# Trainium2 case: five late stages of a transformer kernel turned from waited-for passes into streams, with a new threshold search and one-hot tables

## The reference, cut to what matters

```python
x = x + ffn2(_layernorm(x))     # h = gelu(x @ tern(W_fc).T), exact gelu; LN(h)*w+b; @ tern(W_proj).T
                                # 128 -> 512 -> 128; tern(W) = sign(W)*min(round(|W|/mean|W|), 1)
x = x + xattn3(_layernorm(x))   # softmax((x @ W + b) @ y^T) @ y, y = 64 context rows per batch
x = x + ffn3(_layernorm(x))     # below; 8 experts, 128 -> 512 -> 128

route_prob = jax.nn.softmax(xf @ Ws + bs, axis=-1).T      # [8, 4096]
route_vals, routes = jax.lax.top_k(route_prob, 512)       # each expert takes 512 tokens
h = jax.nn.gelu(jnp.einsum('ekd,edf->ekf', xf[routes], W1) + b1[:, None, :])
out = (jnp.einsum('ekf,efd->ekd', h, W2) + b2[:, None, :]) * route_vals[..., None]
final = zeros.at[routes.reshape(-1)].add(out.reshape(-1, D))
```

## Time and profile before

| what | value |
|---|---|
| median of 3 runs (lowest to highest) | 5028.88 us (5028.64 to 5030.45) |
| profiled execution, its own time | 5030.85 us |
| its span, first to last instruction | 5029.1 us |
| granted TensorE clock, mean | 0.918 |
| busy: PE, DVE, ACT, POOL | 84%, 73%, 56%, 44% |

### The profile page before, as it was taken

One profiled execution on the slowest core, in us unless ns is written; L12 is line 12 of the kernel. 1 busy time (PEld: TensorE's weight loads), 2 busy tenths in 40 slices (PEclk: granted clock), 3 DMA queues, 4 the chain that ended last, 5 costly groups with the idle time before them and its releaser, 6 DMA issues. The chain is left out here.

```text
span 5029.1 us, 113839 instructions
## 1 busy us (share of the span) xinstructions
PE 4220.7 (84%) x40234; PEld 2422.8 (48%) x40619; DVE 3670.4 (73%) x8812; ACT 2816.3 (56%) x5023; POOL 2236.8 (44%) x1403
## 2 busy tenths in 40 slices
PE   8969999999999999999999999999999546456426
PEld 5635555545555555555554555555555325244314
DVE  7878878878888888888887887888887453554440
ACT  3436666666666666666666666666666455342001
POOL 0026555555555555555555555555555001300025
PEclk9989999999999999999999999999999668685558
DMA  1023222322232222322223222232222000000202
GB/s 38 1 67 68 53 59 56 75 60 58 54 77 58 60 56 57 77 56 58 59 54 76 62 55 58 55 76 59 58 54 54 16 11 1 5 0 9 68 6 29
DMA packets 186665, 245.77 MB, mean 49 GB/s; under 512 B 88549, under 2 KB 129255, under 8 KB 186088
## 3 DMA queue, kind: packets, MB, share of 16 engines
q1 hardware_dynamic: 180904, 239.95, 20.5%
q0 software_dynamic: 5632, 4.33, 0.7%
HBM read 41.13 MB, written 14.30 MB: 11 GB/s over the span
## 5 line engine op out<-in xcount | busy, mean ns | idle before, releaser
L1229 POOL TENSOR_TENSOR f_rot_a<-f_rot_a,f_norm 128x1024 f32<-128x1024 f32 x384 | 730.9, 1903 | 1107.1 <-DVE f_norm L1072 1074.6
L1221 POOL TENSOR_TENSOR f_rot_a<-f_rot_a,f_rot_b 128x1024 f32<-128x1024 f32 x384 | 907.5, 2363 | 353.7 <-issue 298.3
L830 PE MATMUL f_bank<-f_w_vo,f_xs_t 128*64 128x512 f32 x3072 | 828.4, 617 | 9.6 <-ACT f_vo L1297 9.6
L1297 ACT ACTIVATE f_vo<-f_bank 128x512 f32<-128x512 f32 x768 | 457.6, 596 | 579.0 <-PE f_bank L830 572.7
L1288 ACT ACTIVATE f_squares<-f_bank 128x512 f32<-128x512 f32 x768 | 459.2, 598 | 330.1 <-PE f_bank L817 244.5
L1051 DVE TENSOR_TENSOR f_rot_a<-f_bank,f_rot 128x512 f32<-128x512 f32 x768 | 527.6, 687 | 85.9 <-POOL f_rot_a L1221 41.7
L1054 DVE TENSOR_TENSOR f_rot_b<-f_bank,f_rot 128x512 f32<-128x512 f32 x768 | 515.1, 671 | 0.0
L863 PE MATMUL f_bank<-f_k_t,f_q_t 128*32 128x128 f32 x12288 | 415.1, 276 | 77.5 <-issue 47.7
L1058 DVE TENSOR_REDUCE f_sums<-f_squares 128x16 f32<-128x1024 f32 x384 | 465.4, 1212 | 3.1
L1100 DVE TENSOR_REDUCE f_stat<-f_score 128x8 f32<-128x512 f32 x384 | 262.1, 682 | 280.2 <-ACT f_score L1314 280.2
L1309 ACT ACTIVATE f_k_t<-f_bank 64x512 f32<-64x512 f32 x768 | 450.5, 587 | 4.8 <-PE f_bank L852 0.3
(11 more groups left out here) (445 smaller groups left out, 7251.6 us busy)
## 6 DMA issues: line engine op xcount, KB each, us to landing
f_vo_off<-f_vo SPq DMA_DIRECT2D x1152, 128.0 KB, 2.3
f_vo_off<-f_vo SPq DMA_DIRECT2D x384, 64.0 KB, 2.0
f_w_qk<-in_Wqk SPq DMA_DIRECT2D x12, 512.0 KB, 5.4
f_vo_dram<-f_vo_pair SPq DMA_DIRECT2D x48, 128.0 KB, 1.8
f_x_shifted<-s_all SPq DMA_DIRECT2D x48, 128.0 KB
f_x_shifted<-s_all SPq DMA_DIRECT2D x48, 127.0 KB
f_w_vo<-f_vo_dram SPq DMA_DIRECT2D x10, 512.0 KB, 3.9
e_w<-in_e_W SPq DMA_DIRECT2D x2, 2048.0 KB
```

The costliest lines, as they stand in the source:

```text
L830: done = nc.tensor.matmul(bank[V][64 * n:64 * n + 64, :], x, w_vo[:, 4 * g:4 * g + 4, n, :], start=True, stop=True)
L1221: nc.gpsimd.tensor_tensor(rot_a[:, slot, :, :], rot_a[:, slot, :, :], rot_b[:, g, :, :], ALU.add).then_inc(rot_summed, 1)
L1229: nc.gpsimd.tensor_tensor(heads, heads, over(norm[:, 16 * g:16 * g + 16], [128, 16, HEAD_DIM]), ALU.mult).then_inc(qk_normed, 1)
L1297: nc.scalar.activation(vo[:, g, 2 * (t % 2) + j, :], flat(V), ACT.Copy).then_inc((va_copied, vb_copied)[j], 1)
```

## The change

`ternary_ffn` is unrolled into one stream. The statistics and roots of `x` are taken first, in two groups of four passes; ScalarE normalises. In step i TensorE turns x(i), does up(i-1), down(i-3) and turns h(i-2). `h` has three buffers and is normalised in place, two tiles on ScalarE and two on VectorE.

`context_attention` and `route` become `attend_and_route`, one stream in which route runs seven steps behind; the copy by GpSimd is gone, and the table's rows are written from ScalarE's output. The roots for route come in two groups, after passes 3 and 7.

`choose` turns the probabilities, so that a partition holds tokens of one expert and has its own attempt; one instruction compares and counts. The one-hot columns are written one at a time against constants, all by VectorE. `apply_experts` has five `taken` buffers: 20 gathers first, then two beside each expert's four adds.

```diff
...
+            def up(p):
+                pe.wait_ge(xn_t_made, p + 1)
+                for t in range(PASS_TILES):
+                    if p > 0:
+                        pe.wait_ge(gelued, PASS_TILES * (p - 1) + t + 1)
+                    nc.tensor.matmul(bank[1 + t][:, :], tile(xn_t[:, p % 2, :], t), w_tern[:, 0, :], start=True, stop=True).then_inc(h_done, 1)
...
+            def turn_h(p):
+                pe.wait_ge(normed_by_vector, p + 1)
+                pe.wait_ge(normed_by_scalar, p + 1)
...
+                    if K * p + k >= 2:
+                        pe.wait_ge(hn_t_made, K * p + k - 1)
+                    to = bank[5 + k % 2]
+                    for t in range(PASS_TILES):
+                        last = nc.tensor.transpose(tile(to, t), h[:, p % 3, t, 128 * k:128 * k + 128], ident[:, :])
+                    last.then_inc(h_turned, 1)
...
+            for i in range(PASSES + 3):
+                if i < PASSES:
+                    turn_x(i)
+                if 1 <= i <= PASSES:
+                    up(i - 1)
+                if 3 <= i:
+                    down(i - 3)
+                if 2 <= i <= PASSES + 1:
+                    turn_h(i - 2)
...
+            def roots_of_h(p):
+                s = p % 2
+                for t in range(PASS_TILES):
+                    dve.wait_ge(gelued, PASS_TILES * p + t + 1)
+                    chain.mark(nc.vector.bn_stats(h_stats[:, s, t, :], h[:, p % 3, t, :]))
+                chain.wait()
+                for t in range(PASS_TILES):
+                    chain.mark(nc.vector.bn_aggr(h_mv[:, s, t, :], h_stats[:, s, t, :]))
+                chain.wait()
+                if p >= 2:
+                    dve.wait_ge(normed_by_scalar, p - 1)
+                chain.link(nc.vector.tensor_scalar(h_var[:, s, 0, :], h_mv[:, s, :, 1], 1e-5, None, ALU.add))
+                chain.link(rsqrt(nc.vector, chain, h_var[:, s, 1, :], h_var[:, s, 0, :], h_var[:, s, 2, :]))
+                nc.vector.scalar_tensor_tensor(h_shift[:, s, :], h_mv[:, s, :, 0], -1.0, h_var[:, s, 1, :], ALU.mult, ALU.mult).then_inc(h_rooted, 1)
+                for t in range(2, PASS_TILES):
+                    last = nc.vector.tensor_scalar(h[:, p % 3, t, :], h[:, p % 3, t, :], h_mv[:, s, t, 0:1], h_var[:, s, 1, t:t + 1], ALU.subtract, ALU.mult)
+                    if t < PASS_TILES - 1:
+                        chain.mark(last)
+                chain.wait()
+                last.then_inc(normed_by_vector, 1)
...
+            for i in range(1, PASSES + 4):
+                if i <= PASSES:
+                    roots_of_h(i - 1)
+                if 3 <= i <= PASSES + 2:
+                    add(i - 3)
...
+            def norm_h(p):
+                act.wait_ge(h_rooted, p + 1)
+                for t in range(2):
+                    last = nc.scalar.activation(h[:, p % 3, t, :], h[:, p % 3, t, :], ACT.Identity, bias=h_shift[:, p % 2, t:t + 1], scale=h_var[:, p % 2, 1, t:t + 1])
+                last.then_inc(normed_by_scalar, 1)
+            def copy_h(p):
+                if p >= 2:
+                    act.wait_ge(o_done, p - 1)
+                for k in range(K):
+                    act.wait_ge(h_turned, K * p + k + 1)
+                    nc.scalar.activation(hn_t[:, p % 2, k, :], bank[5 + k % 2][:, :], ACT.Identity, scale=affine[:, 0, k:k + 1], bias=affine[:, 1, k:k + 1]).then_inc(hn_t_made, 1)
+            act.wait_ge(loaded, 48)
...
+            for i in range(PASSES + 2):
+                if i < PASSES:
+                    copy_x(i)
+                if 2 <= i <= PASSES + 1:
+                    norm_h(i - 2)
+                if 1 <= i <= PASSES:
+                    gelu(i - 1)
+                if i + 2 < PASSES:
+                    norm_x(i + 2)
+                if 2 <= i <= PASSES + 1:
+                    copy_h(i - 2)
...
+            for i in range(PASSES + LAG + 1):
+                if i < PASSES:
+                    turn_x(i)
+                if 1 <= i <= PASSES:
+                    scores(i - 1)
+                if 2 <= i <= PASSES + 1:
+                    turn_s(i - 2)
+                if i < PASSES:
+                    project(i)
+                if LAG <= i < PASSES + LAG:
+                    turn_r(i - LAG)
+                if 2 <= i <= PASSES + 1:
+                    attend(i - 2)
+                if LAG < i:
+                    route(i - LAG - 1)
...
+            def add(p):
+                chain.wait()
+                dve.wait_ge(o_done, p + 1)
+                for t in range(PASS_TILES):
+                    x = tile(of_pass(x_all, p), t)
+                    chain.mark(nc.vector.scalar_tensor_tensor(x, tile(o_bank[p % 2], t), stat[:, p % 2, 2, t:t + 1], x, ALU.mult, ALU.add))
+                chain.wait()
+                nc.vector.nop().then_inc(x_added, 1)
+                take_stats(R, p)
...
+            for i in range(1, PASSES + LAG + 2):
+                if i <= PASSES:
+                    soften(i - 1)
+                if 2 <= i <= PASSES + 1:
+                    invert(i - 2)
+                    add(i - 2)
+                    if (i - 2) % Q == Q - 1:
+                        roots(R, (i - 2) // Q)
+                if LAG < i <= PASSES + LAG:
+                    soften_route(i - LAG - 1)
+                if LAG + 2 <= i:
+                    weigh_route(i - LAG - 2)
...
+            def norm(k, p, to):
+                act.wait_ge(rooted[k], p // Q + 1)
+                for t in range(PASS_TILES):
+                    at = PASS_TILES * p + t
+                    last = nc.scalar.activation(tile(to, t), tile(of_pass(x_all, p), t), ACT.Identity, bias=shift[:, k, at:at + 1], scale=var[:, k, 1, at:at + 1])
+                last.then_inc(tiles_normed[k], 1)
...
+            for i in range(PASSES + LAG + 2):
+                if i < PASSES:
+                    copy_x(i)
+                if 1 <= i <= PASSES:
+                    exponent(i - 1)
+                if i + 1 < PASSES:
+                    norm_x(i + 1)
+                if 2 <= i <= PASSES + 1:
+                    copy_s(i - 2)
+                if i < PASSES:
+                    copy_proj(i)
+                if LAG <= i < PASSES + LAG:
+                    norm(R, i - LAG, of_pass(rn, i - LAG))
+                    copy_r(i - LAG)
+                if LAG < i <= PASSES + LAG:
+                    exponent_route(i - LAG - 1)
...
+            pe.wait_ge(same_made, 1)
+            for i in range(TOP_BIT + 1):
+                pe.wait_ge(counted, i + 1)
+                nc.tensor.matmul(bank[0][:, 0:1], spread[:, :], part[:, :], start=True, stop=True).then_inc(distance_done, 1)
+            pe.wait_ge(found, 1)
+            nc.tensor.transpose(bank[6][:, 0:EXPERTS], attempt[0:EXPERTS, :].bitcast(F32).broadcast_to([EXPERTS, 128]), ident[0:EXPERTS, 0:EXPERTS]).then_inc(threshold_turned, 1)
             pe.wait_ge(tables, 1)
...
+            pe.wait_ge(tile_placed, LOW)
+            pe.wait_ge(row_placed, LOW)
+            pe.wait_ge(high_made, HIGH)
             for h in range(2):
...
                 for t in range(TILES):
                     for e in range(4):
...
+            chain.link(nc.vector.memset(attempt[:, :], 2 ** TOP_BIT))
+            dve.wait_ge(prob_t_made, 1)
+            for i in range(TOP_BIT + 1):
+                bit = 2 ** (TOP_BIT - i)
+                nc.vector.tensor_scalar(over_t[:, :], prob_t[:, :], attempt[:, :].bitcast(F32), -float(CAPACITY // PARTS), ALU.is_ge, ALU.add,
+                                        accum_out=part[:, :]).then_inc(counted, 1)
+                dve.wait_ge(distance_done, i + 1)
+                chain.link(nc.vector.tensor_scalar(change[:, :], bank[0][:, 0:1], float(bit // 2), float(bit + bit // 2), ALU.max, ALU.min))
+                last = nc.vector.tensor_tensor(attempt[:, :], attempt[:, :], change[:, :], ALU.bitwise_xor)
+                if i < TOP_BIT:
+                    chain.link(last)
+            last.then_inc(found, 1)
+            dve.wait_ge(threshold_turned, 1)
+            chain.link(nc.vector.tensor_copy(threshold[:, :], bank[6][:, 0:EXPERTS]))
+            limit = per_tile(threshold[:, :])
...
+            dve.wait_ge(tile_numbered, 1)
+            for n in range(LOW):
+                nc.vector.scalar_tensor_tensor(placed[:, 0, n, :, :], low[:, :, :], float(n + 1), tile_no[:, :, :], ALU.is_equal, ALU.mult).then_inc(tile_placed, 1)
+            for n in range(LOW):
+                nc.vector.tensor_scalar(placed[:, 1, n, :, :], low[:, :, :], float(n + 1), counts[:, TILES:TILES + 1], ALU.is_equal, ALU.mult).then_inc(row_placed, 1)
+            for n in range(HIGH):
+                nc.vector.tensor_scalar(high_hot[:, n, :, :], high[:, :, :], float(n), None, ALU.is_equal).then_inc(high_made, 1)
...
+    RING, PARTS = 5, CAPACITY // 128
+    BESIDE = 2
...
+            def gather(i):
+                e, c = i // PARTS, i % PARTS
+                if c == 0 and e >= RING:
                     pool.wait_ge(x_turned, e - RING + 1)
```

(39 more changed lines are left out.)

552 lines of the change are left out of this document (248 added, 304 removed).

## The result

The changed kernel took 4843.47 us (median of 4 runs, 4842.14 to 4845.76) against 5028.76 beside it: a ratio of 0.9637, 95% interval 0.9626 to 0.9649. The forecast was 4831, range 4802 to 4866. 185.3 us came off where 197.7 were forecast; between the two profiled executions it was 187.9.

What follows compares the result with a forecast made beforehand. The prediction took hand-offs between engines, none of them full, to bound the changed stages. Its terms, -71.6 - 57.5 - 43.2 - 3.1 - 22.3 = -197.7, took 5028.9 to 4831 us, range 4802 to 4866.

Steps and rivals of the forecast that it cites:

- Ternary stage: Ternary feed-forward as one stream: TensorE dense at full clock, steps of 10.6 us, 112.1 against 183.7, so -71.6 us.
- Context and route: Context attention and route merged: steps of 8.0, then 7.9 us for route alone, 141.0 against 198.5, so -57.5 us.
- part of the time: Context steps of the merged stream: TensorE's clock should come up for some of it, hence 8.0 us per step.
- rival B: Merged stream of context and route: TensorE gets full clock, steps of 7.5 and 5.1, -25 us to 4806; chance 0.2.
- Search and columns: Threshold search at 1.74 us per bit, -43.2 us, and one-hot columns, -3.1 us.
- D: The search's single compare-and-count instruction on VectorE: taken as 0.62 us, a 0.424 compare plus a separate 0.201 accumulator reading.
- The columns: One-hot columns on VectorE: 15.7 us of operations, 2.5 of products, 0.5 of outputs, 18.7 in all, so -3.1 us.
- Experts: Experts' stage: two gathers per expert put GpSimd at 10.2 us, below TensorE's 10.79, so rows follow at 10.79.
- the term of 22.3: Experts' stage: the last rows start at 4985.7 where they started at 5008.06, so -22.3 us.

Runs made afterwards that it cites:

- The filler: Sixteen unused turns of the identity added behind each TensorE step from 8 to 14 of the merged stream, against the changed kernel: 4851.03 us (ratio 0.9644).

## Why the prediction was right, and where its terms were off

**Ternary stage, held**: steps of 10.13 for 10.6. `down` at full clock was 3.57 from start to start and turn_h with its wait 2.69 for 2.6; TensorE's one wait was for ScalarE's copies, but ScalarE was not nearly full: busy 7.5 per step for 9.6, since copies by the affine took 0.77 each for 0.84 and the others start before the one ahead has ended. Undoing the stage confirmed the size.

**Context and route, held**: context steps were 7.2 to 8.2 at first, between turns of x, for 8.0, then 7.6 to 10.6 where roots and route's norms joined; the two that hold context's end were 10.5 each for 10.6 and 11.7, and route alone 7.3 for 7.9. The granted clock was 0.65 over 4501.6 to 4535.1, as "part of the time" had it, and 0.50 in route alone; rival B did not come. The filler shows that more work on TensorE raises it.

**Search and columns, too little**: the step was 1.55 for 1.74. The term for D was 0.62 and measured 0.48: the reading did not come on top of the pass, it lay within it. The rest of the bit was 1.07 for 1.12, with small operations of 0.16. The Trainium skill, "VectorE: DVE Perf Modes", section "Two Vector instructions with no wait between them", has the accumulator's reading as an instruction of its own; the trace agrees, with a row of 0.083 for each 0.479, though the two overlap. The columns came out at 19.5 for 18.7, near the forecast only because two errors met, which is luck: VectorE took 13.0 for 15.7, and the strided products 6.1 for 2.5. The Trainium skill, "VectorE: DVE Perf Modes", section "The perf-mode tier table", has tensor_scalar on bf16 in SBUF at four elements and on fp32 at two: rows here have 0.215 for bf16 in and out, starts 0.138 apart, against 0.294 in f32, so the trace agrees in direction. The two-source operations here, at 0.416 in bf16, gained nothing over f32's 0.424; they are SCALAR_TENSOR_TENSOR, which that table does not list.

**Experts, the step that failed**: "With two gathers it has 10.2, below" 10.79, so "rows follow at 10.79". I compared GpSimd's rate with TensorE's and did not ask when each gather is due. Five buffers put 20 gathers ahead, but two per expert behind adds that wait for that expert's rows brings the last pair of expert 7 after rows 5, where TensorE wants it. It cost 12.9 + 2.1 of waits and 5 of clock, 20 us, so that the term of 22.3 came out at 2.6. Three beside the adds took the waits away, and two ahead of them all but 2.1 us.

Between the profiled executions 187.9 us came off for 197.7: the experts missed 19.7, and the other stages gained 9.8 over their terms, 4.8 of it in the search and columns and 1.1 ahead of the five stages. The remaining 2.6 of the 12 us between forecast and time is the difference between profiled executions and medians. That the total came so near is in part luck: one mechanism out of five failed, and errors of the other sign covered half of it.

## What to carry to other kernels

For work in one in-order queue, write down for each item when it is due and what stands ahead of it, and for each of those what it waits for: a rate below the consumer's is not enough, and a lead of buffers is used up where each refill is tied to a late consumer. A stream brings what the densest engine leaves, here steps at full clock where TensorE was the bound, and less where a loop through three engines stays. When columns are laid out for one engine, look at the reads of the next: 512-byte strides doubled the products' time. And when a new effect shows in some runs and not in others, ask first whether those runs share a chip: the stall did.

## What the runs showed of the hardware

- TensorE's instructions dribbled, 0.7 us or a multiple apart and with nothing waited for, from some 25 us after the start of an unbroken run of gathers until 3 to 5 us behind its end. On chip 2 this cost 20 us to the first rows with 32 gathers, 3.7 with 20, and nothing with 12. It was there with 20 or 22 in all six kernels on chips 2 and 12 and in neither on chip 1. The cause is open.
- A TENSOR_SCALAR of 128x256 f32 that counts took 0.479, and its reading of 0.083 ended with it, against 0.294 for one that does not count, and 1.03 for a compare and a reduce.
- Products of two 128x32 bf16 operands took 9.6 ns each with operands side by side and 21 with elements 512 bytes apart, both at a granted clock of 0.50.
- Seven unused turns between dependent products brought TensorE from 1.2 to 2.4 GHz: product from 0.59 to 0.38 us, and 0.20 us less per bit.
